# Attention phase of a sandwich layer: statistics of x behind the next head's maximum, one raw copy of x on VectorE, half of the rounding of x from GpSimd to ScalarE

## The chip, the cores and the metric

The kernel runs on one core of a Trainium2 chip. The metric is the device time of one execution in microseconds (us); lower is better. Before the change it was 1600.59 us, the median of three runs (1599.22 to 1600.85).

## The reference

x has the shape (8, 512, 1024) in float32. Two blocks are computed one after the other, each with a layernorm in front, a layernorm behind and a residual. Cut to what matters:

```
x = x + layernorm(attention(layernorm(x), w_qkv, b_qkv, w_o, b_o))
x = x + layernorm(ffn(layernorm(x), W, b, A, B, gate_w, gate_b))

attention: qkv = x @ w_qkv.T + b_qkv         # 8 heads of 64 columns
           scores[f, t] = k[f] . q[t], where f <= t, else -10000
           attn = softmax(scores, over f);  vals = attn.T @ v
           out = vals @ w_o.T + b_o
ffn:       out = x @ W.T + b + the low-rank product of the rank that the gate picks
```

All products are wanted in float32 accuracy.

## The kernel before

**Two phases.** The attention phase computes q, k, v, the softmax and the values of all eight batch rows and stores them. The output phase follows with the output projection and the ffn. The change touches the attention phase only. Its weights stay on the chip; it treats the eight batch rows one after the other, rows 0 to 6 in a loop body and row 7 in a copy of the body without the work for the next row. The loop body takes 112.7 us.

**High and low parts.** A float32 operand is split into a rounded high part (suffix `h`, hi) and a remainder (suffix `l`, lo), and each product is made as high x high, high x low and low x high. So whatever TensorE transposes (x, the probabilities) or produces (q, k, v) is first rounded, mostly by ScalarE (`p_hi`, `q_hi`, `k_hi`, `v_hi`, `x_high`), and then VectorE forms the remainder (`p_lo`, `q_lo`, `k_lo`, `v_lo`, `x_low`). TensorE can't go on with a bank or an operand until both are done.

**Slots.** The body goes through ten slots, h = 0 to 9, and every engine has the same slots in a queue of its own; the engines meet by semaphores alone. In slot h TensorE makes the scores of head h (`scores`; for heads 1, 2, 3, 6 and 7 already at the end of the slot before, for head 4 behind the first projection step), a projection step of q, k or v (`BETWEEN`; half a step is 12 matmuls), the product of head h-2 with v (`values`), and the transposes of the probabilities of head h-1 in four parts (`transpose_p(h-1, 0)` to `(h-1, 3)`; the last is a small matmul for the masked part). VectorE finds the maximum of head h (`scores_max`), adds up the values of head h-2 (`vals_sum`), makes the remainders of head h-1 (`p_lo`, three parts), the reciprocal of head h's denominators and the remainders of the projections. ScalarE takes the exponentials of head h (`exps`), GpSimd normalises them (`normalise`). `transpose_p(h-1, 2)` needs the first `p_lo` of head h-1, and part 3 the second, since they reuse the two banks `ps_t`.

**The next row's x.** While row b is computed, x of row b+1 is loaded in four tiles t of 128 tokens, each normalised in place: VectorE takes its statistics (`layernorm_stats(t)`, in slots 0 to 3, at the end of the slot), GpSimd normalises it (`layernorm(t)`, behind `normalise` of head t). TensorE transposes each half g of each tile (`transpose_x(t, g)`) into a bank that the projections use too. The order is `TURNED`: in slot 2 (0,0) and (0,1), in slot 3 (1,0), (1,1) and (2,0), in slot 4 (2,1), (3,0) and (3,1). Each of these has a place in the slot: 0 is ahead of `values`, 1 is behind the first two parts of `transpose_p`, 2 is behind the second projection step. A transposed half is copied raw over the place it came from (`x_back`, ScalarE, L712), which frees the bank for the next (semaphore `x_raw`). The bank order makes (1,1) wait for the copy of (1,0), and (2,0) for the copy of (1,1).

**The split of x.** In slot 5, once the last projection of row b has read xTh and xTl (semaphore `x_read` for the k chunks 0 to 3, `q_full` for chunks 4 to 7), the raw copies are split into xTh and xTl: g = 0 is the first half of the chunks, g = 1 the second. ScalarE rounds tiles 0 and 1 (`x_high`, L721) and VectorE forms their remainders (`x_low`, L547). GpSimd does both for tiles 2 and 3 (`split_x`, L467 to L471). The first projection of row b+1 (`project("k", 0, b+1)`) reads chunks 0 to 3 at the end of slot 5 and chunks 4 to 7 at the start of slot 6; at each half it waits for `x_lo_dve` and `x_lo_pool`.

Order on VectorE in slot 5: `scores_max(5)`, `x_low(0)`, `q_lo(3)`, `x_low(1)`, `vals_sum(3)`, `p_lo(4, 0)`, `p_lo(4, 1)`, `reciprocal(5)`, `p_lo(4, 2)`. Order on ScalarE: `x_high(0)`, `exps(5)`, `q_hi(3)`, `x_high(1)`, `vals_lo_part(3)`, `p_hi(4, 0)`, `p_hi(4, 1)`, and the rest.

Of the kernel before, what the change touches and what calls it, by code (L numbers as in the profile page):

```python
# [16 lines left out]
ALU = mybir.AluOpType  # L17
ACT = mybir.ActivationFunctionType
AX = mybir.AxisListType
F32 = mybir.dt.float32  # L20
# [57 lines left out]
def attention_phase(nc, x, wqkvT, bqk, bv, valsT, wl_late, vals_stored, ps_o, W, woT, bo, wagT, BT):  # L78
# [56 lines left out]
    with ExitStack() as ctx:  # L135
        def sb(name, shape, dt, c=ctx):
            return c.enter_context(nc.sbuf_tensor(name, shape, dt))
# [41 lines left out]
        mhalf = sb("mhalf", [P, 1], F32)  # L179
        mone = sb("mone", [P, 1], F32)  # L180
        eps = sb("eps", [P, 1], F32)
        hold = sb("hold", [1, 8], F32)
        nm = sb("nm", [P, 2, 4], F32)
        acc = sb("acc", [P, 2, 4], F32)
        wm = sb("wm", [P, 2, 4], F32)
# [116 lines left out]
        def x_turned(t, b, g):  # L302

            return x_half(t, b, g).rearrange("p (k t) -> p k t", k=4)

        def x_place(xT, t, g):

            return xT[:, 4 * g:4 * g + 4, t * P:(t + 1) * P]
# [113 lines left out]
        def _(pool):  # L422
# [34 lines left out]

            def split_x(g, b):

                if g == 0:  # L460
                    pool.wait_ge(x_read, b)
                else:
                    pool.wait_ge(q_full, 4 * b)
                for t in (2, 3):
                    n = 4 * b + 2 * g + t - 5
                    pool.wait_ge(x_raw, 8 * b - 7 + 2 * t + g)
                    pool.tensor_tensor(hold[:, 2 + 2 * g + t:3 + 2 * g + t], mone[0:1, :], mone[0:1, :], ALU.mult)  # L467
                    pool.tensor_scalar(x_place(xTh, t, g), x_turned(t, b, g), 1.0, 1.0, ALU.mult, ALU.mult)\
                        .then_inc(x_hi_pool, 1)
                    pool.wait_ge(x_hi_pool, n)  # L470
                    pool.tensor_tensor(x_place(xTl, t, g), x_turned(t, b, g), x_place(xTh, t, g).bitcast(F32),  # L471
                                       ALU.subtract).then_inc(x_lo_pool, 1)

# [50 lines left out]
        def _(dve):  # L524
            def layernorm_stats(t, b):
                q = t % 2
                dve.wait_ge(x_landed[t], 16 * (b + 1))
                if not (isinstance(b, int) and 4 * b + t < 2):

                    dve.wait_ge(xn_ready, 4 * b + t - 1)  # L530
                for i in range(2):
                    dve.bn_stats(stats[:, q, 6 * i:6 * i + 6], x_half(t, b, i))

                dve.drain()
                dve.bn_aggr(mv[:, q, :], stats[:, q, :]).then_inc(mv_ready, 1)

            def x0_low(t):
                for g in range(2):
                    dve.wait_ge(x0_hi, 2 * t + g + 1)
                    dve.tensor_tensor(x_place(xTl, t, g), x0_bank(t, g)[:, :].rearrange("p (k t) -> p k t", k=4),  # L540
                                      x_place(xTh, t, g).bitcast(F32), ALU.subtract).then_inc(x_lo_dve, 1)

            def x_low(g, b):

                for t in range(2):
                    dve.wait_ge(x_hi_act, 4 * b + 2 * g + t - 3)
                    dve.tensor_tensor(x_place(xTl, t, g), x_turned(t, b, g), x_place(xTh, t, g).bitcast(F32),  # L547
                                      ALU.subtract).then_inc(x_lo_dve, 1)

            def p_lo(h, g, b):  # L550
                o, n = PT_GROUP[g]
                dve.wait_ge(t_hi, 3 * (8 * b + h) + g + 1)
                dve.tensor_tensor(PTl[:, o:o + n], ps_t[g % 2][:, 0:n], PTh[:, o:o + n].bitcast(F32),  # L553
                                  ALU.subtract).then_inc(t_lo, 1)
# [25 lines left out]
            def scores_max(h, b):  # L580
                H, q = 8 * b + h, h % 2


                dve.wait_ge(held, 1 + H)
                dve.wait_ge(s_done, H + 1)
                dve.memset(hold[:, 0:1], 0.0).then_inc(held, 1)

                m = maskf[:, :].bitcast(U32)
                diag = ps_s[:, 384:1536].rearrange("p (i c) -> p i c", c=384)[:, :, 0:P]
                dve.copy_predicated(diag, m.unsqueeze(1).to_broadcast([P, 3, P]),  # L590
                                    masked[:, :].unsqueeze(1).to_broadcast([P, 3, P])).then_inc(mask_done, 1)
                dve.copy_predicated(ps_s[:, 896:1024], m, masked[:, :].to_broadcast([P, P])).then_inc(mask_done, 1)
                dve.wait_ge(mask_done, 2 * H + 2)
                for i in range(NT):
                    last = dve.tensor_reduce(nm[:, q, i:i + 1], ps_s[:, S_OFF[i]:S_OFF[i] + (i + 1) * P],
                                             AX.X, ALU.max, negate=True)
                last.then_inc(max_done, 1)
                dve.wait_ge(max_done, H + 1)

                dve.tensor_scalar(nm[:, q, 0:3], nm[:, q, 0:3], -MASKED, None, ALU.min).then_inc(nm_ready, 1)  # L600
# [40 lines left out]
            def body(b, last):  # L641
                for h in range(SLOTS):
                    if h < NH:
                        scores_max(h, b)
                    if h == X_SLOT and not last:
                        x_low(0, b + 1)
                    if h in SOON:
                        lows(h, 0, b, last)
                    if h == X_SLOT and not last:
                        x_low(1, b + 1)  # L650
                    if last and h == 9:
                        first_attention_out()
                    if h >= 2:
                        vals_sum(h - 2, b)
                    if 1 <= h <= NH:
                        for g in range(2):
                            p_lo(h - 1, g, b)
                    if h < NH:
                        reciprocal(h, b)
                    if h not in SOON:  # L660
                        lows(h, 0, b, last)
                    lows(h, 1, b, last)
                    if 1 <= h <= NH:
                        p_lo(h - 1, 2, b)
                    if last and h == 6:
                        first_vals_low()
                    if last:
                        for n in SPLITS.get(h, ()):
                            next_low(n)
                    if not last:  # L670
                        if h < 4:
                            layernorm_stats(h, b + 1)

            def split_w(n):
                dve.wait_ge(w_hi, n + 1)
# [26 lines left out]
        def _(act):  # L702
# [11 lines left out]
            def x_high(g, b):  # L714

                if g == 0:
                    act.wait_ge(x_read, b)
                else:
                    act.wait_ge(q_full, 4 * b)
                for t in range(2):  # L720
                    act.activation(x_place(xTh, t, g), x_turned(t, b, g), ACT.Copy).then_inc(x_hi_act, 1)  # L721

            def p_hi(h, g, b):
# [60 lines left out]
            def backs(h, place, b, last):  # L784
                for t, g in turned(h, place, last):
                    x_back(t, g, b + 1)

            def body(b, last):
                for h in range(SLOTS):


                    late = h == BEHIND or last and h >= BARE
                    if h == X_SLOT and not last:
                        x_high(0, b + 1)
                    backs(h, 0, b, last)
                    if h < NH and not late:
                        exps(h, b)
                    if h in SOON:
                        highs(h, 0, b, last)
                    if h == X_SLOT and not last:  # L800
                        x_high(1, b + 1)
                    if h >= 2:
                        vals_lo_part(h - 2, b)
                    if 1 <= h <= NH:
                        for g in range(2):
                            p_hi(h - 1, g, b)
                    backs(h, 1, b, last)
                    if h < NH and late:
                        exps(h, b)
                    if h not in SOON:  # L810
                        highs(h, 0, b, last)
                    backs(h, 2, b, last)
                    highs(h, 1, b, last)
                    if last and h == NH:
                        for n in POOL_SPLITS:
                            next_high(n)
                    if 1 <= h <= NH:
                        p_hi(h - 1, 2, b)
                        masked_spread(h - 1, b)
                    if last and h == 9:  # L820

                        act.wait_ge(first_scale, 1)
                        act.activation(W.z[:, :], W.y[:, :], ACT.Identity, scale=W.rstd[:, 0:1], bias=W.shift[:, 0:1])
                    if last and h == 6:
                        first_vals_high()
                    if last:
                        for n in SPLITS.get(h, ()):
                            next_high(n)
# [703 lines left out]
```

## Time and profile before

| | before |
|---|---|
| runs, median (lowest to highest) | 1600.59 us (1599.22 to 1600.85) |
| the profiled execution: its time, its span | 1594.81 us, 1593.0 us |
| TensorE (PE) busy | 1510.6 us, 95% |
| VectorE (DVE) busy | 977.5 us, 61% |
| ScalarE (ACT) busy | 692.9 us, 43% |
| GpSimd (POOL) busy | 627.1 us, 39% |
| granted TensorE clock, mean | 0.973 |

The span is the time from the first to the last instruction of the profiled execution. PE is TensorE's matmuls, PEld its weight loads beside them. A row of the time line has the start, the busy time, the engine, the line of the kernel, the operation, output and input, and how many instructions were merged; in square brackets stands how long the engine was idle before it and what it waited for. The program's names for x's tiles are mixed in the trace: x and xs are both x, and `ps_o` is the pair of banks that projections and transposed x share.

### The profile page before, as it was taken

Reading aid. Unit: us, or ns where it says so; the run is one execution under the profiler, and the core shown is the slowest. Engines: PE = TensorE matmul, PEld = TensorE weight load, DVE = VectorE, ACT = ScalarE, POOL = GpSimd, SP = SyncE. Lnnn points to the kernel's source line nnn. Section 1 sums busy time; section 2 is a strip of 40 time slices with the busy share of each in tenths; the row PEclk is TensorE's granted clock in tenths of the full one; section 3 lists DMA queues with packets and bytes.
Section 4 is the critical chain, followed back from the end, with each engine's and each line's share of the span. In section 5 each row is a group of like instructions: output and inputs, shape, how many; then the busy total and the mean of one; then the engine's idle time right before and its main releaser. Section 6 shows DMA issues by size and latency. Waiting matters only on the chain. (4 is left out here: it accounts for less than half of the span.)

```text
span 1593.0 us, 25018 instructions
## 1 busy us (share of the span) xinstructions
PE 1510.6 (95%) x8032; PEld 1325.6 (83%) x8032; DVE 977.5 (61%) x2105; ACT 692.9 (43%) x1492; POOL 627.1 (39%) x1184
## 2 busy tenths in 40 slices
PE   7989989999999999999899869999999999999996
PEld 5878878778878878878788659999999999999996
DVE  7475565575664665655654666666666666666663
ACT  5454464554563553644544552333333333333331
POOL 2352451452452452533522453444444444444443
PEclk9999999999999999999999979999999999999998
DMA  6212103112112112121110441211111111211110
GB/s 238 70 34 76 49 23 92 33 44 68 33 49 63 36 49 72 36 53 59 36 53 20 145 160 34 67 66 66 66 66 66 66 66 66 66 66 66 66 60 40
DMA packets 46927, 102.93 MB, mean 65 GB/s; under 512 B 5040, under 2 KB 21424, under 8 KB 46896
## 3 DMA queue, kind: packets, MB, share of 16 engines
q1 hardware_dynamic: 46896, 102.54, 20.6%
q8 instruction: 16, 0.26, 0.1%
q14 instruction: 15, 0.12, 0.0%
HBM read 60.06 MB, written 25.69 MB: 54 GB/s over the span
## 5 line engine op out<-in xcount | busy, mean ns | idle before, releaser
L1456 PE MATMUL ps_f<-wagh,x2Th 128*128 128x364 f32 x768 | 256.4, 334 | 4.4 <-DVE f L1318 2.9
L1456 PE MATMUL ps_f<-wagl,x2Th 128*128 128x364 f32 x768 | 253.5, 330 | 0.0
L1456 PE MATMUL ps_f<-wagh,x2Tl 128*128 128x364 f32 x768 | 253.0, 329 | 0.0
L913 PE MATMUL ps_o<-xTh,wh 128*128 128x512 f32 x504 | 210.8, 418 | 3.3 <-DVE xTl L540 2.1
L913 PE MATMUL ps_o<-xTh,wl 128*128 128x512 f32 x504 | 204.2, 405 | 0.0
L913 PE MATMUL ps_o<-xTl,wh 128*128 128x512 f32 x504 | 204.1, 405 | 0.0
L1456 PEld LDWEIGHTS ps_f<-wagh,x2Th 128*128 128x128 f32 x768 | 145.5, 189 | 7.2 <-issue 5.0
L440 POOL TENSOR_TENSOR cw<-wm,cnt 128x4 f32<-128x4 f32 x64 | 15.9, 248 | 341.3 <-ACT pr L759 341.3
L1456 PEld LDWEIGHTS ps_f<-wagl,x2Th 128*128 128x128 f32 x768 | 145.6, 190 | 1.3
L1456 PEld LDWEIGHTS ps_f<-wagh,x2Tl 128*128 128x128 f32 x768 | 145.3, 189 | 0.0
L611 DVE SCALAR_TENSOR_TENSOR vt<-ps_v,bv_s,vt 64x512 f32<-64x512 f32 x64 | 47.6, 743 | 155.2 <-ACT vt L768 154.7
L1189 POOL TENSOR_TENSOR var_eps<-mv,eps 128x1 f32<-128x1 f32 x95 | 19.1, 201 | 300.2 <-DVE mv L1252 300.2
L447 POOL TENSOR_SCALAR pr<-pr,rden 128x128 f32<-128x128 f32 (+3 forms) x256 | 136.5, 552 | 0.0
L759 ACT ACTIVATE pr<-ps_s,nm 128x128 f32<-128x128 f32 (+3 forms) x256 | 130.4, 520 | 0.1
L553 DVE TENSOR_TENSOR PTl<-ps_t,PTh 128x512 fp32r<-128x512 f32 (+1 forms) x192 | 109.5, 598 | 19.2 <-ACT PTh L726 16.2
L913 PEld LDWEIGHTS ps_o<-xTh,wh 128*128 128x128 f32 x504 | 99.5, 198 | 25.3 <-ACT xs L712 2.7
L1357 ACT ACTIVATE zf<-f,shift,rstd 128x512 f32<-128x512 f32 x64 | 48.7, 808 | 164.9 <-POOL shift L1193 164.9
L726 ACT ACTIVATE PTh<-ps_t 128x512 fp32r<-128x512 f32 (+1 forms) x192 | 94.2, 527 | 55.2 <-PE ps_t L976 53.0
L913 PEld LDWEIGHTS ps_o<-xTh,wl 128*128 128x128 f32 x504 | 99.2, 197 | 22.8
L1303 DVE TENSOR_TENSOR x2Tl<-ps_x,x2Th 128x512 fp32r<-128x512 f32 x64 | 43.6, 691 | 119.3 <-ACT x2Th L1377 118.9
L976 PE MATMUL ps_t<-ident,pr 128*128 128x128 f32 x640 | 93.3, 277 | 23.6 <-DVE PTl L553 21.4
L913 PEld LDWEIGHTS ps_o<-xTl,wh 128*128 128x128 f32 x504 | 99.7, 198 | 18.2
(170 smaller groups left out, 3590.5 us busy)
## 6 DMA issues: line engine op xcount, KB each, us to landing
kst<-kst SPq DMA_DIRECT2D x64, 256.0 KB, 3.6
xt<-in_x SPq DMA_DIRECT2D x32, 512.0 KB, 4.0
out<-outs SPq DMA_DIRECT2D x32, 512.0 KB, 3.1
xs<-in_x SPq DMA_DIRECT2D x24, 512.0 KB, 4.4
valsT<-vt SPq DMA_DIRECT2D x64, 128.0 KB, 2.3
vraw<-valsT SPq DMA_DIRECT2D x32, 256.0 KB, 4.2
raw<-in_wqkvT SPq DMA_DIRECT2D x12, 512.0 KB, 5.7
wag_raw<-in_wagT SPq DMA_DIRECT2D x8, 546.0 KB, 5.8
```

What stands on the lines that cost most here:

```text
L440: pool.tensor_tensor(cw[:, q, :], wm[:, q, :], cnt[:, :], ALU.mult).then_inc(cw_done, 1)
L447: last = pool.tensor_scalar(at, at, rden[:, q, i:i + 1], 1.0, ALU.mult, ALU.mult)
L553: dve.tensor_tensor(PTl[:, o:o + n], ps_t[g % 2][:, 0:n], PTh[:, o:o + n].bitcast(F32), ALU.subtract).then_inc(t_lo, 1)
L611: dve.scalar_tensor_tensor(out=vt[0:HD, :], in0=ps_v[0:HD, :], scalar=bv_s[:, h:h + 1], in1=vt[HD:P, :], op0=ALU.add, op1=ALU.add).then_in ...
L726: act.activation(PTh[:, o:o + n], ps_t[g % 2][:, 0:n], ACT.Copy).then_inc(t_hi, 1)
L759: last = act.activation(pr[:, q, S_OFF[i]:S_OFF[i] + n], ps_s[:, S_OFF[i]:S_OFF[i] + n], ACT.Exp, bias=nm[:, q, i:i + 1], accum_out=acc[:, ...
L913: done = pe.matmul(ps[:, :], w[:, k, c:c + P], xT[:, k, :], start=(k == 0 and w is wh and xT is xTh), stop=(k == KD - 1 and w is wl), skip ...
L976: last = pe.transpose(ps_t[bank][:, at - o:at - o + P], pr[:, h % 2, S_OFF[i] + j * P:S_OFF[i] + (j + 1) * P], ident[:, :])
L1189: pool.tensor_tensor(var_eps[:, c:c + 1], mv[:, c, 1:2], eps[:, :], ALU.add)
L1303: dve.tensor_tensor(x2Tl[:, 4 * g:4 * g + 4, :], ps_x[:, g, :].rearrange("p (k t) -> p k t", k=4), x2Th[:, 4 * g:4 * g + 4, :].bitcast(F32 ...
L1357: return act.activation(out_, in_, ACT.Identity, scale=rstd[:, c:c + 1], bias=shift[:, c:c + 1])
L1456: last = pe.matmul(ps_f[:, g, 0:GW], a[:, k, :], w[:, k, cols], start=(k == 0 and a is x2Th and w is wagh), stop=False, skip_group_check=True)
```

## The change

Four edits in the loop body.

1. `layernorm_stats(0)`, `(1)` and `(2)` move from the end of slots 0, 1 and 2 to slots 1, 2 and 3, behind `scores_max` of that slot. `layernorm_stats(3)` stays at the end of slot 3.
2. The raw copy of the half (1,1) moves from ScalarE, where it stood behind `p_hi(2, 1)` in slot 3, to VectorE, ahead of `vals_sum(1)` and `p_lo(2, 0)`.
3. For g = 0, ScalarE rounds all four tiles, ahead of `exps(5)`; GpSimd only forms the remainders of tiles 2 and 3. For g = 1 the work is split as before.
4. `x_low(1)` moves on VectorE from behind `q_lo(3)` to behind `vals_sum(3)`, `p_lo(4, 0)` and `p_lo(4, 1)`.

```diff
 # GpSimd, split_x(g, b)
-                if g == 0:
-                    pool.wait_ge(x_read, b)
-                else:
-                    pool.wait_ge(q_full, 4 * b)
                 for t in (2, 3):
...
-                    pool.tensor_scalar(x_place(xTh, t, g), x_turned(t, b, g), 1.0, 1.0, ALU.mult, ALU.mult)\
-                        .then_inc(x_hi_pool, 1)
-                    pool.wait_ge(x_hi_pool, n)
+                    if g == 0:
+                        pool.wait_ge(x_hi_act, 6 * b + t - 5)
+                    else:
+                        pool.wait_ge(q_full, 4 * b)
+                        pool.wait_ge(x_raw, 8 * b - 6 + 2 * t)
+                        pool.tensor_tensor(hold[:, 2 + t:3 + t], mone[0:1, :], mone[0:1, :], ALU.mult)
+                        pool.tensor_scalar(x_place(xTh, t, g), x_turned(t, b, g), 1.0, 1.0, ALU.mult, ALU.mult)\
+                            .then_inc(x_hi_pool, 1)
+                        pool.wait_ge(x_hi_pool, 2 * b + t - 3)
                     pool.tensor_tensor(x_place(xTl, t, g), x_turned(t, b, g), x_place(xTh, t, g).bitcast(F32),
                                        ALU.subtract).then_inc(x_lo_pool, 1)
 # VectorE
+            def x_back(t, g, b):
+
+                dve.wait_ge(x_full, 8 * b - 7 + 2 * t + g)
+                dve.tensor_copy(x_half(t, b, g), ps_j[X_BANK[t, g]][:, :]).then_inc(x_raw, 1)
 # VectorE, body(b, last)
                     if h < NH:
                         scores_max(h, b)
+                    if 1 <= h <= 3 and not last:
+                        layernorm_stats(h - 1, b + 1)
                     if h == X_SLOT and not last:
                         x_low(0, b + 1)
                     if h in SOON:
                         lows(h, 0, b, last)
-                    if h == X_SLOT and not last:
-                        x_low(1, b + 1)
+                    if h == 3 and not last:
+                        x_back(1, 1, b + 1)
...
                     if 1 <= h <= NH:
                         for g in range(2):
                             p_lo(h - 1, g, b)
+                    if h == X_SLOT and not last:
+                        x_low(1, b + 1)
...
-                        if h < 4:
-                            layernorm_stats(h, b + 1)
+                        if h == 3:
+                            layernorm_stats(3, b + 1)
 # ScalarE, x_high(g, b)
-                for t in range(2):
+                for t in range(4 if g == 0 else 2):
+                    act.wait_ge(x_raw, 8 * b - 7 + 2 * t + g)
                     act.activation(x_place(xTh, t, g), x_turned(t, b, g), ACT.Copy).then_inc(x_hi_act, 1)
 # ScalarE, body(b, last)
-                    backs(h, 1, b, last)
+                    if h != 3:
+                        backs(h, 1, b, last)
```

The semaphore counts that depend on `x_hi_act` change with it (six per row, before four), and the scratch tile `hold` shrinks from 8 to 6 elements.

## Rows read from the trace of the kernel before

**Rows 1.** The waits: engine, line, releaser: us in total, times, longest us

```profile
PE ps_t L976 <- DVE PTl L553: 21.4, 11, 2.5
...
PE ps_o L878 <- ACT xs L712: 15.0, 7, 2.2
...
PE ps_t L970 <- DVE PTl L553: 2.7, 17, 0.2
```

**Rows 2.** TensorE's time line, slot 3 and the start of slot 4 of row 2

```profile
312.02 0.39 PE L913 MATMUL ps_o<-xTh,wl 128*128 128x512 f32 x1
314.54 0.67 PE L878 MATMUL ps_o<-ident,xs 128*128 128x128 f32 x4 [2.14 <-ACT xs L712]
...
315.90 0.79 PE L913 MATMUL ps_o<-xTh,wh 128*128 128x512 f32 x1
...
318.56 0.39 PE L913 MATMUL ps_o<-xTh,wh 128*128 128x512 f32 x1
```

**Rows 3.** Windows: stretch, length, busy PE, PEld, DVE, ACT, POOL, PE clock, DMA, GB/s

```profile
315.00:318.00 3.00, 3.00 (x10) 2.27 (x9) 1.01 (x4) 2.61 (x5) 2.22 (x5) 0.51 0.19 44
...
877.00:880.00 3.00, 3.00 (x17) 2.62 (x16) 0.95 (x2) 0.00 (x0) 1.90 (x3) 1.00 0.00 0
```

**Rows 4.** TensorE's time line in row 7

```profile
875.17 0.44 PE L976 MATMUL ps_t<-ident,pr 128*128 128x128 f32 x2 [0.91 <-DVE PTl L553]
```

**Rows 5.** VectorE's time line, slot 3

```profile
305.55 1.27 DVE L532 BATCH_NORM_STATS2 stats<-xs 128x6 f32<-128x512 f32 x2
...
307.10 0.06 DVE L586 MEMSET hold<- 1x1 f32 x1
...
313.02 0.74 DVE L611 SCALAR_TENSOR_TENSOR vt<-ps_v,bv_s,vt 64x512 f32<-64x512 f32 x1 [3.11 <-ACT vt L768]
313.79 1.29 DVE L553 TENSOR_TENSOR PTl<-ps_t,PTh 128x512 fp32r<-128x512 f32 x2
...
317.14 1.51 DVE L560 SCALAR_TENSOR_TENSOR qst<-ps_o,bqk_s,qst 64x512 fp32r<-64x512 f32 x2 [1.98 <-ACT qst L736]
```

**Rows 6.** ScalarE's time line, slot 3

```profile
309.94 0.30 ACT L756 ACTIVATE wm<-nm,masked 128x3 f32<-128x3 f32 x1 [2.68 <-DVE nm L600]
...
315.75 1.36 ACT L736 ACTIVATE qst<-ps_o,bqk_s 64x512 fp32r<-64x512 f32 x2
```

**Rows 7.** GpSimd's time line, slot 3

```profile
308.20 1.19 POOL L433 TENSOR_SCALAR xs<-xs,nmean,rstd 128x1024 f32<-128x1024 f32 x1 [0.18 <-issue]
```

**Rows 8.** Groups of instructions: count, then busy us and mean ns of one

```profile
L447 POOL TENSOR_SCALAR pr<-pr,rden 128x128 f32<-128x128 f32 (+3 forms) x256 | 136.5, 552 | 0.0
```

**Rows 9.** TensorE's time line, end of slot 5 and slot 6

```profile
337.82 0.47 PE L913 MATMUL ps_o<-xTh,wh 128*128 128x512 f32 x1
...
344.29 0.44 PE L976 MATMUL ps_t<-ident,pr 128*128 128x128 f32 x2 [2.19 <-DVE PTl L553]
...
349.50 0.40 PE L991 MATMUL ps_v<-PTh,v 128*128 128x512 f32 x1
```

**Rows 10.** VectorE's time line, slot 5

```profile
334.69 1.85 DVE L547 TENSOR_TENSOR xTl<-xs,xTh 128x512 fp32r<-128x512 f32 x2
...
339.97 2.77 DVE L547 TENSOR_TENSOR xTl<-xs,xTh 128x512 fp32r<-128x512 f32 x2
...
343.55 1.29 DVE L553 TENSOR_TENSOR PTl<-ps_t,PTh 128x512 fp32r<-128x512 f32 x2
```

**Rows 11.** ScalarE's time line, slot 5

```profile
332.47 1.16 ACT L721 ACTIVATE xTh<-xs 128x512 fp32r<-128x512 f32 x2 [1.78 <-PE ps_o L913]
334.81 0.30 ACT L756 ACTIVATE wm<-nm,masked 128x3 f32<-128x3 f32 x1 [1.18 <-DVE nm L600]
...
339.59 0.60 ACT L768 ACTIVATE vt<-ps_v 64x512 f32<-64x512 f32 x1
```

**Rows 12.** GpSimd's time line, slot 5

```profile
340.58 1.61 POOL L471 TENSOR_TENSOR xTl<-x,xTh 128x512 fp32r<-128x512 f32 x1
```

**Rows 13.** GpSimd's time line in row 7

```profile
908.74 5.04 POOL L447 TENSOR_SCALAR pr<-pr,rden 128x128 f32<-128x128 f32 x4
```

More of the change, by code:

```diff
@@ L181, in attention_phase @@
         eps = sb("eps", [P, 1], F32)
-        hold = sb("hold", [1, 8], F32)
+        hold = sb("hold", [1, 6], F32)
         nm = sb("nm", [P, 2, 4], F32)
@@ L458, in split_x @@
             def split_x(g, b):
-                if g == 0:
-                    pool.wait_ge(x_read, b)
-                else:
-                    pool.wait_ge(q_full, 4 * b)
                 for t in (2, 3):
-                    n = 4 * b + 2 * g + t - 5
-                    pool.wait_ge(x_raw, 8 * b - 7 + 2 * t + g)
-                    pool.tensor_tensor(hold[:, 2 + 2 * g + t:3 + 2 * g + t], mone[0:1, :], mone[0:1, :], ALU.mult)
-                    pool.tensor_scalar(x_place(xTh, t, g), x_turned(t, b, g), 1.0, 1.0, ALU.mult, ALU.mult)\
-                        .then_inc(x_hi_pool, 1)
-                    pool.wait_ge(x_hi_pool, n)
+                    if g == 0:
[7 more added lines that the diff above has]
+                        pool.wait_ge(x_hi_pool, 2 * b + t - 3)
                     pool.tensor_tensor(x_place(xTl, t, g), x_turned(t, b, g), x_place(xTh, t, g).bitcast(F32),
@@ L541, in x0_low @@
                                       x_place(xTh, t, g).bitcast(F32), ALU.subtract).then_inc(x_lo_dve, 1)
+            def x_back(t, g, b):
+                dve.wait_ge(x_full, 8 * b - 7 + 2 * t + g)
+                dve.tensor_copy(x_half(t, b, g), ps_j[X_BANK[t, g]][:, :]).then_inc(x_raw, 1)
             def x_low(g, b):
                 for t in range(2):
-                    dve.wait_ge(x_hi_act, 4 * b + 2 * g + t - 3)
+                    dve.wait_ge(x_hi_act, 6 * b + 4 * g + t - 5)
                     dve.tensor_tensor(x_place(xTl, t, g), x_turned(t, b, g), x_place(xTh, t, g).bitcast(F32),
```

## The prediction

> **What bounds the kernel now.** I read the waits first, TensorE's own [rows 1]. In the attention phase it waits for little, but always for the same: 7 times for a copy of x by ScalarE (15.0 us together) and 11 times for the remainder PTl of the probabilities (21.4 us). Both come once in each of the seven loop rows; all other waits of the loop are small. So TensorE bounds, and two stalls a row of some 2.2 us are what can be had. Next comes the time line of row 2, which repeats in the others.
>
> Stall 1: in slot 3 TensorE issues the last matmul of a projection at 312.02, could turn the half (2,0) one step of 0.23 later, at 312.25, and does so at 314.54 [rows 2]. It waits for the raw copy of (1,1), which ScalarE makes only behind the exponentials of head 3, the copy of its low values and two PTh. Stall 2 is in slot 5, until 344.29, for the first PTl of head 4 [rows 9].
>
> Each stall costs more than its wait. After stall 1 the granted clock is 0.51 for 315 to 318 [rows 3], the lower level of 1.2 GHz, where it was 2.4 GHz before: seven matmul steps (first at 315.90, full speed again at 318.56) go in 0.44 each instead of 0.23 [rows 2]. After stall 2 the twelve matmuls in front of 349.50 are slow in the same way [rows 9]. A wait of 0.91 in row 7 [rows 4] left the clock at 1.00 [rows 3]. So a stall that shrinks below 1 us gives back its slow matmuls too.
>
> **The change, part by part.** Times are those of row 2 before.
>
> *Statistics behind the maximum.* In slot 3 VectorE spends 305.55 to 307.10 on statistics before scores_max(3) starts [rows 5]: 1.55. Now the maximum comes first, so exps(3) starts at 308.4 instead of 309.94 [rows 6], and all that hangs on it: p_lo(2,0) followed the exponentials' start by 3.85 (313.79 less 309.94), so it starts at 312.25, ends about 0.7 later at 312.95, and p_lo(2,1) ends at 313.55. In slots 1 and 2 the same happens, but TensorE waited for nothing there: worth nothing. The price: the statistics end 2.85 later (the length of scores_max, 307.10 to 309.94). From their start to x normalised took 3.84 (305.55 to 308.20 + 1.19 on GpSimd [rows 5, 7]); now 308.4 + 3.84 = 312.24, just when TensorE wants tile 2, at 312.25. No slack, no cost; I allow 0.1.
>
> *Raw copy on VectorE.* The half (1,1) is turned ahead of the twelve matmuls that end at 312.02, so by about 309.7. VectorE comes to the copy behind maximum and statistics, at 309.95. No row has such a copy. Of VectorE's operations that read 512 columns of PSUM, PTl has 0.6 a step and vals_sum 0.74 [rows 5]; a copy has one operand less than either, so these are its bounds from above, and half of 0.6 would be one from below. I take 0.7: it ends at 310.65. Behind it stands vals_sum(1), which waits for ScalarE until 313.02 - 1.54 = 311.5 [rows 5]: covered, even at 1.5 us. The bank is free at 310.7, long before 312.25: stall 1 as it was is gone. What is late next is PTl: transpose_p(2,2) could go at 312.60 and goes at 313.0, the masked product (which needs p_lo(2,1)) at 313.6, and the next projection's first matmul at 313.9. ScalarE copies (2,0) in time (turned by 312.9, copied by 313.55). Full speed assumed, its seventh matmul is at 313.9 + 6 x 0.23 = 315.28, before it was at 318.56 [rows 2]: **3.28 gained a row**. Two covers of it are thin. scores(4) needs q_lo(2): q_hi starts at 313.55 and q_lo 1.39 later [rows 5, 6], ends at 316.45; TensorE comes at 316.66. And x's tile 3, normalised by 320.6, is wanted at 320.9. Either one missed costs tenths.
>
> *Four roundings on ScalarE.* x_high(0) starts at 332.47 and took two steps of 0.58; with four it ends at 334.8. exps(5) starts at 334.81 [rows 11], since it waits for the maximum: ScalarE was idle for those 1.18. It fits with nothing to spare. Bounds: 0 to 0.1 a row, I take 0; without that cover it would be 1.16 on everything behind. GpSimd loses two roundings and two one-element operations, but starts its remainders at 334.3, when ScalarE has done tile 2. They now run beside x_low(0) of VectorE (334.69 [rows 10]). A pair of x_low took 1.85 at one place and 2.77 at the other, where the 1.61 of GpSimd's remainder ran beside it [rows 10, 12]: they hold each other up. If all four went one by one, they would end at 334.3 + 2 x 1.61 + 1.85 = 339.4, which is 1.6 behind 337.82, where TensorE starts on them [rows 9]; if nothing collides, at 337.5. I take 338.1, and the wait below absorbs it.
>
> *x_low(1) behind PTl.* ScalarE's order for g = 1 is unchanged, so vals_sum(3) still has its input from 339.59 + 0.72 = 340.3 (the copy's 0.60 [rows 11] and 0.1 until VectorE sees it). Before, x_low(1) filled 339.97 to 342.74 [rows 10]. Now p_lo(4,0) starts at 341.1 instead of 343.55, ends at 341.75, and p_lo(4,1) ends at 342.4. TensorE, done with scores(6) at about 342.1, doesn't wait for the first and 0.3 for the second. But x_low(1) starts only then, and the first projection's second half, which TensorE could start at 342.7, needs it. It is two operations of 0.93 (1.85 for the pair), or less, 0.68 each, where GpSimd is quiet, and it should be: its last remainder ends at 342.2 [rows 12]. I take 1.35 (near the short end, because nothing reads beside it; the bounds are 1.3 and 2.77): end at 343.7. So a wait of 1.0 takes the place of one of 2.2, under the size that lowered the clock. Twelve matmuls at 0.23 later, values(4) starts at 346.47, before 349.50 [rows 9]: **3.03 gained**.
>
> The Trainium skill (SBUF — State Buffer, "Who interferes with whom") says that a VectorE instruction with two SBUF inputs and a GpSimd one that reads SBUF exclude each other for a whole instruction. The pairs of 1.85 and 2.77 fit that. By this rule the price of x_low(1) is a matter of where GpSimd stands, which is the first rival.
>
> *Given back.* Behind it TensorE is 3.03 early, while the exponentials of head 6 are only some 1.2 early. The slack of slot 6 takes that up, but in slot 7, where a wait for PTl of 0.16 stands already [rows 1], I allow another 0.15.
>
> **Sum.** 3.28 + 3.03 - 0.15 = 6.16 a row, times seven loop rows = 43 us. Row 7 and the output phase have none of it. Against the profiled execution's own time, 1594.81 (span 1593.0 and 1.8 around it), that is 1552. The median of the runs is 5.8 above that execution, for reasons that a profile doesn't show; I count from the median: 1600.6 - 43 = **1557**.
>
> **The rivals.**
> (a) x_low(1) merely takes stall 2's place. If GpSimd is late by a microsecond, the pair takes 2.77: 342.35 + 2.77 = 345.1, the second half starts when it did, and the clock falls as before. Only 3.28 a row stays: 23 us, **1578**. For it: the 2.77; against: GpSimd's work there ends before VectorE starts. 14%.
> (b) The waits shrink, but the clock falls all the same. The waits left are 0.8 around 313 and 1.4 around 342; the known cases are 0.91 (no fall) and 2.2 (fall). Slow matmuls cost 7 x 0.2 = 1.3 at the one and 3.0 - 1.46 = 1.6 at the other place. Both: 3.3 a row, 23 us, also **1578**; the second alone: 4.6 a row, 32 us, 1568. Together 16%, half of it the milder one.
> (c) The split and the copies meet no waits at all: stalls gone fully: at the first the wait of 2.29, the 0.74 by which 314.54 to 315.90 is longer than 0.62 at full speed, and 1.28 of slow matmuls; at the second 2.2, 0.3 and 1.6, 8.4 a row, 59 us, **1542**. Against it: x_low(1) has to run somewhere. 4%.
> (d) The change doesn't do what it says, because stall 1 has a second cause just behind the copy (tile 2 normalised late: GpSimd waits for statistics that come 2.85 later). If tile 2 came 2 us behind my 312.24, stall 1 would stay and 3.0 a row be left, 1579; if stall 2 stayed too, the time would be the **same**. 4% for the latter.
> (e) Slower: GpSimd becomes the pace. In slots 1 to 3 its layernorm now waits for the later statistics and stands in front of the next head's normalise. It may be some 2.9 late before the transposes wait. Its four pr of a head took 5.04 once in row 7 [rows 13] against 4 x 0.55 = 2.2 in the mean [rows 8]; were that so here, it would be 2.85 + 2.85 = 5.7 late at each of three heads, 2.8 a head or 8.4 a row lost, against 6.16 gained: 7 x 2.24 = 16 us slower, **1616**. It decides from 2.9 + 6.16/3 = 5.0 us late. Against it: GpSimd is busy for only 39% of the span, and 5.04 stands only in row 7, which this change leaves as it is. 4%.
>
> **How the numbers follow.** My forecast 58%, with a range of its own of 1551 to 1566 (the thin covers above it, a shorter pair below); (a) 14, (b) 16, (c) 4, (d) 4, (e) 4. Range 1548 to 1579: it takes in (a), (b) and the bounds. A measurement tells 0.2%, 3 us, from no change. Faster by more: 92%; within: 4%; slower: 4%.
>
> **What would show it.** Right: TensorE's wait for ScalarE's xs is gone from the list; the wait for PTl falls from 21.4 to under 8 us, a new one for VectorE's xTl of about 1 us a row stands in slot 6; the clock is at 1.00 in slots 3 to 6; a row takes 106.6 us instead of 112.7. Wrong: waits of TensorE for GpSimd's tile of x ahead of (2,0) or (3,0); x_low(1) at 2.77; a clock of 0.5 behind waits of 1 us; exps(5) later behind x_high(0).

## The result and the profile after

The changed kernel takes 1557.49 us, the median of four runs (1556.79 to 1559.51). The kernel before took 1600.62 beside it. The ratio is 0.973, with a 95% interval of 0.972 to 0.975. A second comparison, five runs against nine of the kernel before, gave 1559.32 against 1599.11, a ratio of 0.975 (0.9735 to 0.9765). The profiled execution took 1556.95, with a span of 1555.1 and a mean granted clock of 0.988, where it was 0.973 before.

Busy time of each engine in the kernel after: us, share of the span, instructions.

```profile
PE 1493.2 (96%) x8032; PEld 1308.3 (84%) x8032; DVE 981.6 (63%) x2112; ACT 696.7 (45%) x1499; POOL 611.5 (39%) x1156
```

TensorE has as many matmuls as before and is busy for 17 us less. So not only waits went: the same matmuls ran faster. Where the waits went is in the list of TensorE's waits (line, releaser: us in total, times, longest) for the loop, 50 to 830 us, after:

```profile
PE ps_o L923 <- DVE xTl L551: 6.7, 14, 0.8
PE ps_t L980 <- DVE PTl L557: 3.3, 21, 0.2
PE ps_t L986 <- DVE PTl L557: 1.6, 7, 0.2
```

ScalarE's xs is gone from the list, and the wait for the first PTl of head 4 is now one of 0.2 [rows 1]. (In the whole execution the wait for PTl at this line is 7.4 now, where it was 21.4; what is left of it lies mostly in row 7, outside the loop.) In their place stands the wait for the remainder of x: 14 times, 0.76 and 0.19 in each row. The granted clock of the loop, stretch by stretch (length, busy PE, PEld, DVE, ACT, POOL, clock, DMA share, GB/s), after:

```profile
50.00:820.00 770.00, 757.73 (x4017) 639.39 (x4016) 480.86 (x1008) 412.00 (x1032) 307.30 (x631) 1.00 0.18 51
...
305.00:308.00 3.00, 3.00 (x17) 2.41 (x16) 2.92 (x5) 0.56 (x2) 1.66 (x3) 1.00 0.00 0
333.00:336.00 3.00, 3.00 (x21) 2.71 (x20) 1.27 (x3) 1.66 (x8) 1.28 (x2) 1.00 0.00 0
```

and behind stall 2 before:

```profile
346.00:349.00 3.00, 3.00 (x9) 2.35 (x8) 2.26 (x7) 0.64 (x4) 2.02 (x4) 0.50 0.00 0
```

The clock is 1.00, 2.4 GHz, in the whole loop, and so at the two places where it had fallen to 0.51 [rows 3] and 0.50: 305 to 308 is what was 315 to 318, and 333 to 336 what was 346 to 349.

A loop row takes 107.21 us, from one (1,0) turned to the next, instead of 112.73. That is 5.52 a row. The first row before took only 111.79, since the clock stayed at 1.00 behind its stall 1, so 37.7 are gained over seven rows; from profile to profile it is 37.9.

**Slot 3.** Row 2 has (1,0) turned 10.09 earlier than before. Add 10.09 to an after time and it stands beside [rows 2], [rows 5] and [rows 6]. TensorE's time line, after:

```profile
302.22 0.65 PE L888 MATMUL ps_o<-ident,xs 128*128 128x128 f32 x4
...
303.82 0.39 PE L923 MATMUL ps_o<-xTh,wh 128*128 128x512 f32 x1
...
306.56 1.53 PE L959 MATMUL ps_s<-kst,qst 128*128 128x128 f32 x8
307.93 0.60 PE L888 MATMUL ps_o<-ident,xs 128*128 128x128 f32 x4
```

VectorE's, ScalarE's and GpSimd's time lines, after:

```profile
298.14 0.17 DVE L604 TENSOR_SCALAR nm<-nm 128x3 f32<-128x3 f32 x1
298.24 1.29 DVE L531 BATCH_NORM_STATS2 stats<-xs 128x6 f32<-128x512 f32 x2
...
299.72 0.68 DVE L545 COPY xs<-ps_o 128x512 f32<-128x512 f32 x1
301.42 0.74 DVE L615 SCALAR_TENSOR_TENSOR vt<-ps_v,bv_s,vt 64x512 f32<-64x512 f32 x1 [1.02 <-ACT vt L777]
302.19 1.29 DVE L557 TENSOR_TENSOR PTl<-ps_t,PTh 128x512 fp32r<-128x512 f32 x2
```

```profile
298.34 0.30 ACT L765 ACTIVATE wm<-nm,masked 128x3 f32<-128x3 f32 x1 [1.16 <-DVE nm L604]
```

```profile
300.89 1.20 POOL L433 TENSOR_SCALAR xs<-xs,nmean,rstd 128x1024 f32<-128x1024 f32 x1 [0.18 <-issue]
```

The exponentials of head 3 start at 298.34, while VectorE has only begun with the statistics. VectorE copies for 0.68 and then is idle for 1.02, tile 2 is normalised at 302.09, and (2,0) is turned at 302.22, 0.29 behind the matmul ahead of it, with no wait that the trace marks.

**Slots 5 and 6.** From here 13.25 is to be added (that is how far scores(5) lies ahead of before). VectorE, ScalarE and GpSimd, after:

```profile
321.19 1.09 DVE L604 TENSOR_SCALAR nm<-nm 128x3 f32<-128x3 f32 x1
322.20 2.37 DVE L551 TENSOR_TENSOR xTl<-xs,xTh 128x512 fp32r<-128x512 f32 x2
...
328.60 1.29 DVE L557 TENSOR_TENSOR PTl<-ps_t,PTh 128x512 fp32r<-128x512 f32 x2
329.81 1.28 DVE L551 TENSOR_TENSOR xTl<-xs,xTh 128x512 fp32r<-128x512 f32 x2
```

```profile
320.79 0.62 ACT L730 ACTIVATE xTh<-x 128x512 fp32r<-128x512 f32 x1
322.32 0.30 ACT L765 ACTIVATE wm<-nm,masked 128x3 f32<-128x3 f32 x1 [0.92 <-DVE nm L604]
...
327.11 0.59 ACT L777 ACTIVATE vt<-ps_v 64x512 f32<-64x512 f32 x1
```

```profile
320.96 1.30 POOL L470 TENSOR_TENSOR xTl<-xs,xTh 128x512 fp32r<-128x512 f32 x1 [2.27 <-ACT xTh L730]
322.22 1.80 POOL L470 TENSOR_TENSOR xTl<-x,xTh 128x512 fp32r<-128x512 f32 x1
```

And TensorE, after:

```profile
324.62 0.50 PE L923 MATMUL ps_o<-xTh,wh 128*128 128x512 f32 x1 [0.19 <-DVE xTl L551]
...
329.35 0.44 PE L986 MATMUL ps_t<-ident,pr 128*128 128x128 f32 x2 [0.23 <-DVE PTl L557]
...
331.14 0.50 PE L923 MATMUL ps_o<-xTh,wh 128*128 128x512 f32 x1 [0.76 <-DVE xTl L551]
...
333.98 0.39 PE L1001 MATMUL ps_v<-PTh,v 128*128 128x512 f32 x1
```

One row stands out. The last step of scores_max, TENSOR_SCALAR L604, works on three elements a partition. In slot 3 it took 0.17, here it took 1.09. In the kernel before (its line is L600 there) the step of slot 5 took 0.32, and it too ended with a remainder of GpSimd's (334.77 and 334.75):

```profile
334.45 0.32 DVE L600 TENSOR_SCALAR nm<-nm 128x3 f32<-128x3 f32 x1
```

```profile
333.46 1.29 POOL L471 TENSOR_TENSOR xTl<-xs,xTh 128x512 fp32r<-128x512 f32 x1
```

So the collision could be seen, small, before the change; the remainder now starts 0.23 ahead of the step and no longer 0.99 ahead, and the step sits out nearly all of it. In the kernel after the step starts while GpSimd forms its first remainder (320.96 to 322.26) and ends with it, within 0.02. The exponentials of head 5 start 0.92 behind the last rounding, with ScalarE idle in between: they wait for this step and not for the four roundings.

### The profile page after: what moved, and what is told of

The parts are those of the page before. It is cut to its first block and busy times, and to the rows that moved or that the text cites. A ratio compares the mean times of both kernels' runs of the same rounds, so it can differ in the third digit from the quotient of the medians.

```text
span 1555.1 us, 25025 instructions
## 1 busy us (share of the span) xinstructions
PE 1493.2 (96%) x8032; PEld 1308.3 (84%) x8032; DVE 981.6 (63%) x2112; ACT 696.7 (45%) x1499; POOL 611.5 (39%) x1156
## 5 line engine op out<-in xcount | busy, mean ns | idle before, releaser
L923 PE MATMUL ps_o<-xTh,wh 128*128 128x512 f32 x504 | 203.4, 404 | 8.8 <-DVE xTl L551 6.7
L923 PE MATMUL ps_o<-xTh,wl 128*128 128x512 f32 x504 | 198.0, 393 | 0.0
L923 PE MATMUL ps_o<-xTl,wh 128*128 128x512 f32 x504 | 197.1, 391 | 0.0
L923 PEld LDWEIGHTS ps_o<-xTh,wh 128*128 128x128 f32 x504 | 95.2, 189 | 28.8 <-DVE xTl L551 10.1
L923 PEld LDWEIGHTS ps_o<-xTh,wl 128*128 128x128 f32 x504 | 95.0, 188 | 21.2
L923 PEld LDWEIGHTS ps_o<-xTl,wh 128*128 128x128 f32 x504 | 95.3, 189 | 16.9
L599 DVE TENSOR_REDUCE nm<-ps_s 128x1 f32<-128x128 f32 (+3 forms) x256 | 107.7, 483 | 2.2
```

The source lines that it names most:

```text
L923: done = pe.matmul(ps[:, :], w[:, k, c:c + P], xT[:, k, :], start=(k == 0 and w is wh and xT is xTh), stop=(k == KD - 1 and w is wl), skip ...
```

## The experiments

Medians are of the runs named; the kernel before, run on the same chip, stands at 1597.21 for the first four (seven runs), 1599.11 for the next four and 1598.75 for the last three (nine runs each). The length of a row is taken from the time lines.

**u4_xlow_early: edit 4 undone.**

```diff
+                    if h == X_SLOT and not last:
+                        x_low(1, b + 1)
                     if last and h == 9:
...
-                    if h == X_SLOT and not last:
-                        x_low(1, b + 1)
```

> Only x_low(1) goes back to its place ahead of vals_sum(3); the other edits stay. Theory: the wait for the first PTl of head 4 is back with 2.7 us (2.2 of before and the 0.5 to 0.76 by which exps(5) is later now), the clock falls behind it, values(4) starts 2.9 us later: 20 us, about 1577. Rival (the four roundings and the early exponentials already removed it): within 3 us of 1557.

1578.4 (1577.42 to 1580.23), ratio 0.989 (0.987 to 0.990); rows of 109.5 to 109.9, one of 110.9, in which the clock stayed low for longer (0.52 still at 450.2 to 453.2, 3.5 us behind the wait). TensorE's wait is back at its old place:

```profile
PE ps_t L986 <- DVE PTl L557: 15.8, 7, 2.3
```

Behind all seven of these waits the granted clock was 0.50 to 0.63 over three us. Edit 4 is worth 2.3 to 2.7 a row with the others in place, and 3.7 in that one: the largest share.

**u1_stats_back: edit 1 undone.**

```diff
-                    if 1 <= h <= 3 and not last:
-                        layernorm_stats(h - 1, b + 1)
...
-                        if h == 3:
-                            layernorm_stats(3, b + 1)
+                        if h < 4:
+                            layernorm_stats(h, b + 1)
```

> Only the move of the statistics is undone (they stand at the end of slots 0 to 3 again); the other three edits stay. Theory (each stall of TensorE is a chain that starts at exps of the head, and the statistics sat in front of the maximum): exps(3) starts 1.55 us later, so p_lo(2,0) and the matmuls behind it too. A wait of about 1.9 us for PTl stands in slot 3 again and the clock falls behind it: 1.54 + 1.2 = 2.7 us a row, 19 us, about 1576; if the clock holds, 11 us, 1568. Rival (what held TensorE was only the place of the copy of (1,1)): no change, 1557.

1575.31 (1570.33 to 1576.89), ratio 0.986 (0.983 to 0.988). TensorE waits 1.7 a row for the first PTl of head 2, in slot 3. Two of these waits on its time line, and the windows behind them:

```profile
311.06 0.44 PE L984 MATMUL ps_t<-ident,pr 128*128 128x128 f32 x2 [1.69 <-DVE PTl L557]
...
419.77 0.44 PE L984 MATMUL ps_t<-ident,pr 128*128 128x128 f32 x2 [1.70 <-DVE PTl L557]
```

```profile
311.60:314.60 3.00, 2.95 (x13) 2.48 (x14) 2.35 (x5) 1.42 (x3) 2.84 (x6) 1.00 0.19 44
420.30:423.30 3.00, 2.94 (x7) 2.41 (x8) 2.35 (x6) 1.43 (x3) 2.83 (x6) 0.53 0.19 44
```

The waits are equal, the clock behind them is not: it fell in three of the seven rows. A row took 108.7 where it stayed and 110.3 where it fell. So edit 1 is worth 1.5 a row, and 3.1 where its absence lowers the clock.

**u2_copy_on_act: edit 2 undone.**

```diff
-                    if h == 3 and not last:
-                        x_back(1, 1, b + 1)
...
-                    if h != 3:
-                        backs(h, 1, b, last)
+                    backs(h, 1, b, last)
```

> Only the copy of (1,1) goes back to ScalarE, behind p_hi(2,1); the other edits stay. Theory: with exps(3) early, ScalarE can copy at 302.3 to 302.9 (times of the changed kernel's row 2), so the half (2,0) is turned 0.7 us later, but the next projection starts only 0.4 us later since PTl is the later input anyway; with the following q_lo 0.4 to 0.6 us a row, 3 to 4 us, about 1561. Rival (the copy is the stall, as the waits of before name it): the wait of 2.1 us and its slow matmuls are back, 3.3 us a row, 23 us, about 1580.

1560.5 (1560.2 to 1561.69), ratio 0.978 (0.976 to 0.979); rows of 107.95, 0.74 longer. With the exponentials early enough ScalarE's copy is nearly in time, and waits of 0.6 and 0.3 are left:

```profile
PE ps_o L885 <- ACT xs L718: 4.4, 7, 0.6
PE ps_o L920 <- ACT xs L718: 2.0, 7, 0.3
```

The copy is what TensorE was seen to wait for in [rows 1], and moving it is the smaller part of the cure.

**u3_pool_rounds: edit 3 undone** (GpSimd rounds tiles 2 and 3 of the first half itself, as before, and needs no ScalarE for it).

```diff
-                    if g == 0:
-                        pool.wait_ge(x_hi_act, 6 * b + t - 5)
...
-                for t in range(4 if g == 0 else 2):
+                for t in range(2):
```

(The diff is cut: `split_x` and the counts of `x_hi_act` are those of the kernel before.)

> Only the four roundings are undone: GpSimd rounds tiles 2 and 3 of g = 0 itself again. Theory: in the changed kernel the last operation of scores_max(5), three elements, takes 1.09 us instead of 0.17, held up by GpSimd's remainder that now starts in front of it, and all of ScalarE's chain of slot 5 is 0.76 us late by that. With GpSimd on its old order that is gone: x_low(1) ends 0.66 us earlier, 0.66 us a row, about 4.5 us faster than the changed kernel, 1553. Rival (the edit does what it is for, GpSimd ends earlier and TensorE waits less in slot 5): 1 to 3 us slower, 1559 to 1560.

1554.86 (1551.81 to 1557.02), ratio 0.974 (0.972 to 0.976); rows of 106.43, 0.78 shorter. **u3_again** is the same kernel again, with five runs.

> The changed kernel without the four roundings once more, beside it on one chip: 106.43 us a row against 107.2, so 5.4 us less in seven rows, if the clock between the two phases is alike.

1555.89 (1553.82 to 1557.33), ratio 0.973 (0.971 to 0.974), rows of 106.44. **after_again**, the changed kernel beside it:

> The changed kernel once more, on the chip of this call, as the measure for the other three: 1556 to 1559, 107.2 us a loop row.

1559.32 (1557.43 to 1560.06), rows of 107.20. The rows differ by 0.75, as expected, which is 5.3 us in seven; the medians differ by 3.4 only, so the rest is lost outside the loop. Edit 3 costs: of the four it is the one that is better left out. In u3_pool_rounds the step of the maximum in slot 5 takes 0.28 to 0.31, near the 0.32 of the kernel before.

**nm_by_reduce: how edit 3 costs.** The last step of scores_max is another operation, which gives the same values: TENSOR_REDUCE over pairs of the maximum and a constant. (The diff is cut: `nmx` is a new tile, filled with the constant, and the maxima are written into it.)

```diff
-                dve.tensor_scalar(nm[:, q, 0:3], nm[:, q, 0:3], -MASKED, None, ALU.min).then_inc(nm_ready, 1)
+                dve.tensor_reduce(nm[:, q, 0:3], nmx[:, q, 0:3, :], AX.X, ALU.min).then_inc(nm_ready, 1)
```

> The changed kernel, but the last operation of the maximum (the smaller of the row maximum and 10000, on three elements) is made by a tensor_reduce over pairs, not by a tensor_scalar from SBUF to SBUF. Theory (the tensor_scalar is held up by GpSimd's remainder because both want the same way into SBUF, and a reduce isn't): the operation takes 0.2 instead of 1.09 in slot 5, exps(5) starts 0.8 us earlier, a row takes about 106.45 us, 5 us less in all. Rival (VectorE is held up whatever it does, or ScalarE's four roundings set exps(5)): 107.2 us a row, no change.

1552.08 (1548.83 to 1552.45), ratio 0.970 (0.9685 to 0.972); rows of 106.32, 0.89 shorter. VectorE and GpSimd in slot 5 of this kernel:

```profile
320.13 0.16 DVE L607 TENSOR_REDUCE nm<-nmx 128x3 f32<-128x6 f32 x1
320.23 3.20 DVE L553 TENSOR_TENSOR xTl<-xs,xTh 128x512 fp32r<-128x512 f32 x2
```

```profile
319.89 1.30 POOL L471 TENSOR_TENSOR xTl<-xs,xTh 128x512 fp32r<-128x512 f32 x1 [2.28 <-ACT xTh L733]
```

GpSimd's remainder has been running for 0.24 when the step starts, as in the kernel after, and the step takes 0.16 all the same. Now it is x_low(0) that is held up, 3.20 for the pair, and that is covered. The mean of all 64 such steps, after (first) and in this kernel (count, then busy us and mean ns of one); besides the 1.09 of slot 5 the first has 0.52 in slot 1 of each row:

```profile
L604 DVE TENSOR_SCALAR nm<-nm 128x3 f32<-128x3 f32 x64 | 20.8, 326 | 2.2
```

```profile
L607 DVE TENSOR_REDUCE nm<-nmx 128x3 f32<-128x6 f32 x64 | 10.2, 159 | 2.2
```

The Trainium skill (SBUF — State Buffer, "Who interferes with whom") has this: VectorE's copies, casts and tensor_scalar can run in modes that take the port pair shared with GpSimd, and a VectorE instruction with two SBUF inputs contends with a GpSimd one that reads SBUF; whoever issues first keeps the pair for the whole instruction, and on trn2 tensor_reduce never contends. The traces agree, with 1.09 and 0.16, and they show that three elements are enough to be caught.

**pool_after_max: the same cost taken away from the other side.** GpSimd starts its first remainder only when the maximum is done.

```diff
                         pool.wait_ge(x_hi_act, 6 * b + t - 5)
+                        if t == 2:
+                            pool.wait_ge(nm_ready, 8 * b - 2)
```

> The changed kernel, but GpSimd starts its remainders of g = 0 only when the maximum of head 5 is done (one wait more). Theory: exps(5) starts 0.8 us earlier, but the remainders end later, beside x_low(0): the projection's first half waits up to 0.8 us more and x_low(1) meets GpSimd again; about 107.0 us a row. Rival (GpSimd doesn't hold up VectorE): exps(5) where it was and the first half 0.8 us later, 107.6 or more.

1549.9 (two runs, 1548.92 and 1550.87), ratio 0.969 (0.967 to 0.9715); rows of 106.34. Slot 5 of this kernel, VectorE and TensorE:

```profile
318.77 0.17 DVE L606 TENSOR_SCALAR nm<-nm 128x3 f32<-128x3 f32 x1
318.88 2.39 DVE L553 TENSOR_TENSOR xTl<-xs,xTh 128x512 fp32r<-128x512 f32 x2
```

```profile
322.54 0.47 PE L925 MATMUL ps_o<-xTh,wh 128*128 128x512 f32 x1 [0.54 <-POOL xTl L472]
```

The step takes its 0.17 again. TensorE now waits 0.54 for GpSimd, but the row is no longer than with the other operation: 107.0 was expected, but x_low(1) met only the last 0.13 of GpSimd's remainder and took 1.28. Two remedies with nothing in common but the cause give rows of 106.32 and 106.34, and leaving the edit out gives 106.43: the cause is shown.

**b1_only_edit1 and b4_only_edit4: each large edit alone on the kernel before** (diffs as in edits 1 and 4).

> The kernel before with edit 1 alone (statistics behind the maximum). Theory (the late exponentials held the copy of (1,1) as well as PTl, so edit 1 does most of the work on stall 1): the wait for xs shrinks from 2.1 to about 0.6 us and its slow matmuls go, 2.5 to 2.7 us a row, 110.1. Rival (the copy's place on ScalarE is the stall): the wait stays, 112.0 or more.

1573.4 (two runs, 1572.75 and 1574.06), ratio 0.984 (0.982 to 0.987); rows of 108.6 and 109.8 in turn, so 4.1 and 2.9 gained, where 2.5 to 2.7 was expected. Its waits:

```profile
PE ps_t L978 <- DVE PTl L553: 15.4, 7, 2.2
PE ps_o L880 <- ACT xs L714: 4.4, 7, 0.6
```

Edit 1 alone takes the wait for the copy from 2.2 to 0.6.

> The kernel before with edit 4 alone (x_low(1) behind vals_sum(3) and the two p_lo of head 4). Theory (the two stalls are chains of their own, and edit 4 alone removes the one in slot 5): that one goes with its slow matmuls, 3.0 us a row, 109.7 instead of 112.73; the wait for ScalarE's xs stays as it is with 15 us. Rival (the gains need each other): under 2 us a row.

1572.62 (two runs, 1571.91 and 1573.32), ratio 0.984 (0.981 to 0.986); rows of 109.7 and 108.8. The wait for the copy stays as it was, and two of these waits read:

```profile
309.64 0.65 PE L878 MATMUL ps_o<-ident,xs 128*128 128x128 f32 x4 [2.17 <-ACT xs L712]
...
418.38 1.12 PE L878 MATMUL ps_o<-ident,xs 128*128 128x128 f32 x4 [2.13 <-ACT xs L712]
```

The four small matmuls took 0.65 behind the one and 1.12 behind the other; the clock of the three us behind them was 1.00 and 0.52. It fell in four of seven rows here, and in three of seven in b1_only_edit1. In the kernel before it fell behind 13 of 14 such waits. Each edit alone gains some 3.5 a row. They sum to 7.0, more than the 5.5 of all four: with one stall gone, the one that is left lowers the clock in about half of the rows only, and the second edit can't gain that again. So 4/7 of a fall's 1.2 (b1_only_edit1) and 3/7 of a fall's 1.0 (b4_only_edit4) are counted twice, 1.1 together. Edit 2's 0.74 comes on, edit 3's 0.78 comes off, so 5.9 would be left; the last 0.4 is not explained.

**reduce_and_high1_late: a further step on nm_by_reduce.** ScalarE forms x_high(1) behind p_hi(4, 1).

```diff
-                    if h == X_SLOT and not last:
-                        x_high(1, b + 1)
...
+                    if h == X_SLOT and not last:
+                        x_high(1, b + 1)
```

> The changed kernel with the three-element operation as a reduce, and with x_high(1) on ScalarE behind p_hi(4,1) instead of ahead of vals_lo_part(3). Theory: the low values and the two PTh of slot 5 come 1.15 us earlier; VectorE, behind q_lo(3), can use 0.4 of that, so the first projection's second half starts 0.4 us earlier: 105.9 us a row, about 1549. Rival (ScalarE isn't in that chain any more): 106.3 a row, 1551.

1551.75 (1550.68 to 1553.12), ratio 0.971 (0.969 to 0.973). Rows are 105.97, 0.35 shorter, or 2.5 us in seven, but the median is the one of nm_by_reduce. The windows between the two phases, of this kernel and of nm_by_reduce:

```profile
840.00:930.00 90.00, 70.78 (x312) 60.19 (x311) 55.15 (x101) 44.72 (x87) 38.35 (x70) 0.77 0.41 135
```

```profile
840.00:930.00 90.00, 68.26 (x321) 57.72 (x320) 57.50 (x104) 45.81 (x92) 38.34 (x70) 0.85 0.41 135
```

There TensorE is busy for 2.5 us more at a clock of 0.77 instead of 0.85. It has the gaps of the change of phase in both kernels. The first (1,0) is turned 1.1 later too (83.36, against 82.27), though the two kernels are the same up to there. Why the clock stays low for longer in the one is open; the like is seen between two executions of one kernel, below.

## Why the prediction was right, and where it was not

**Stall 1: right, step by step.** On the clock of [rows 2] the exponentials of head 3 started at 308.43 (308.4 was said), the copy took 0.68 (0.7), tile 2 was normalised at 312.18 (312.24), (2,0) turned at 312.31 (312.25), the next projection began at 313.91 (313.9) and scores(4) at 316.65 (316.66). Gained by scores(5): 3.16 a row, where 3.28 was said. The tenth was lost at the other cover called thin, q_lo(2) in front of scores(4), and not at tile 3. q_lo(2) ended at 306.33, so the first weights of scores(4) were loaded at 306.55, with its first matmul (306.56) and not 0.22 ahead of it as before. From scores(4) to (2,1) it took 1.37 (306.56 to 307.93), where before it took 1.28:

```profile
319.94 1.44 PE L949 MATMUL ps_s<-kst,qst 128*128 128x128 f32 x8
321.22 0.60 PE L878 MATMUL ps_o<-ident,xs 128*128 128x128 f32 x4
```

**Four roundings on ScalarE: the step that failed.** It was priced at 0, with bounds of 0 to 0.1. The roundings themselves fit as said: done at 334.66 (334.8 was said). But GpSimd's remainders began at 334.21, and one caught the last step of the maximum, so the exponentials of head 5 began at 335.57 instead of 334.81. The prediction weighed that collision for the x_low pair alone, whose delay is hidden, and not for the small operation ahead of it on the same engine, whose delay nothing hides. Its price was 0.78 a row (u3_pool_rounds, where the step keeps its 0.3) to 0.89 (nm_by_reduce, where it takes 0.16). The sign named for this miss, exps(5) later, did show; but the cause is not x_high(0), behind which ScalarE was idle for 0.92.

**x_low(1) behind PTl: right in mechanism, off by that term.** The first PTl of head 4 came at 341.85 (341.1 was said), so 0.75 late, and the pair behind it took 1.28 (1.35). The wait in front of the second half was 0.76 (1.0), but its end was at 344.39, not 343.7. values(4) started at 347.23, 2.27 earlier than in [rows 9], where 3.03 was said.

**Given back: nothing.** 3.16 + 2.27 = 5.43, and a row gained 5.52. The 0.15 was not needed.

**The sum: 6.16 a row was said, 5.52 was measured.** From the profiled execution the sum gave 1552, and the profiled execution after took 1556.95: 5 us off, all of them in the loop (0.64 a row, and 0.9 for the first row, which had only one of its stalls followed by slow matmuls). The prediction of 1557 counted from the median, 5.8 higher, and so met the measured 1557.49: that it is this near is luck, a sum 5 us too large against a base 6 us higher. Between the medians of the first comparison 43.1 were gained, between those of the second 39.8, in the seven rows of the traces 37.7. What the rest of the 43.1 is can't be said, since only one execution of the kernel before has a trace. Executions of it scatter from 1594.6 to 1601.1, and the slower ones have a lower mean clock (0.969 against 0.975). It is not shown that this went with the stalls: in the traced one 13 of 14 had their fall already. The changed kernel scatters as well, and it has two traces, of 1556.95 and 1559.37 us (after and after_again). Their rows are alike, 107.21 and 107.20; but the first (1,0) is turned at 81.51 in the one and 83.28 in the other, and the clock in front of it differs:

```profile
10.00:40.00 30.00, 26.28 (x116) 21.50 (x116) 24.82 (x29) 20.12 (x25) 4.09 (x9) 0.94 0.63 220
```

```profile
10.00:40.00 30.00, 26.52 (x108) 21.56 (x108) 24.35 (x29) 20.10 (x25) 4.18 (x9) 0.89 0.58 196
```

So 1.8 of these 2.4 us come ahead of slot 3 of the first row, in one and the same kernel and without a stall of the two.

**Two readings of rows.** The prediction says that the waits for PTl and for xs come once in each loop row. For xs that is so; of the 11 for PTl 7 lie in the loop, with 15.4 of the 21.4 us, and its sum rightly counts these. And it counts seven steps of 0.44 from 315.90 to 318.56; there are six (2.66), which its 1.28 fits.

**The rivals.** (a) needed x_low(1) at 2.77; it took 1.28, since GpSimd was done. (b) needed the clock to fall behind waits of 1 us; behind 0.76 it stayed at 1.00 in every row, but behind 1.7 it fell in three of seven (u1_stats_back), so the rival lay closer than its own row [rows 4] told. In row 7 of the kernel after it even fell behind two waits of 0.87 and 1.37, which end at 858.97 and 861.38: the clock of the three us behind them is 0.51. In u2_copy_on_act the same two leave it at 1.00. (c) is out, since 0.19 and 0.76 are waited. (d) and (e) are out: tile 2 came on time, and TensorE never waited for GpSimd in the loop.

## What to carry to other kernels

When a step moves to a new neighbour, look at every instruction beside which it now runs on the engines that it can hold up, the smallest first: it is the short one on the critical chain that costs, not the long one that is covered. A step of 0.32 where its like takes 0.17 is a sign of it in the profile before. Follow a wait back past the operation that it names: here the copy was moved, and most of the gain at its stall came from letting the maximum go ahead of the statistics, well before it. And price a wait with what stands behind it: on TensorE waits of 1.7 to 2.2 cost another 1.0 to 1.6 us of slow matmuls wherever the clock fell behind them, waits of 0.76 in the loop cost nothing more.

## What the runs showed of the hardware

- A VectorE TENSOR_SCALAR on three elements took 1.09 us instead of 0.17 beside a GpSimd TENSOR_TENSOR of 128x512 that had started 0.23 ahead of it; a TENSOR_REDUCE with as many results in the same place took 0.16.
- A pair of x_low took 1.28 with GpSimd quiet, 1.85 to 3.20 beside its remainders; GpSimd's own remainder took 1.30 alone and 1.59 to 1.80 beside it.
- Whether TensorE's clock falls is not told by the length of the wait in front alone: behind waits of 2.13 to 2.2 it fell to 1.2 GHz in four of seven rows of one kernel (b4_only_edit4), behind 2.2 in three of seven of another (b1_only_edit1), behind 2.3 in all seven of a third (u4_xlow_early), behind 1.7 in three of seven (u1_stats_back), behind 0.76 in the loop in none. A fall cost 1.0 (b4_only_edit4) to 1.6 us (u1_stats_back).
- Four kernels beat the changed one. Beside its 1559.32 stand u3_again (3.4 us less), nm_by_reduce (7.2) and pool_after_max (9.4); reduce_and_high1_late was run in another comparison and has a ratio of 0.971 against 0.975. The median of pool_after_max is the lowest, but has two runs behind it, so the order of the last three is open.
